# A sparse graph-attention layer: a fifth gather buffer and longer lags between the stages

## The reference

```python
h = jnp.maximum(_layernorm(x), 0.0)                 # x: 8192 x 128 f32
h = h @ W                                           # W: 128 x 128
s_src, s_dst = h @ a[:128, 0], h @ a[128:, 0]
e = leaky_relu(s_src[:, None] + s_dst[None, :], 0.2)
e = jnp.where(adj > 0, e, -9e15)                    # adj: 8192 x 8192 int32, 4 ones a row on average
out = x + softmax(e, axis=1) @ h
```

## Time and profile before

| | us |
|---|---|
| median of 3 timed runs | 804.93 |
| the profiled execution, its span | 858.3 |
| DVE busy | 592.4 (69%) |
| ACT busy | 525.0 (61%) |
| POOL busy | 512.0 (60%) |
| PE busy | 445.4 (52%) |
| adj loads (queue q1), share of the 16 DMA engines | 79.3% |

### The profile page before, as it was taken

The page is one execution under the profiler, slowest core; times in us unless marked ns, Lnnn a source line. Parts: engine busy times, 40 slices in busy tenths (PEclk is TensorE's granted clock), DMA queues, the critical chain, the costliest instruction groups (busy, mean ns, idle before and its releaser), DMA issues.

```text
span 858.3 us, 8941 instructions
## 1 busy us (share of the span) xinstructions
PE 445.4 (52%) x1823; PEld 213.9 (25%) x1855; DVE 592.4 (69%) x3125; ACT 525.0 (61%) x371; POOL 512.0 (60%) x522
## 2 busy tenths in 40 slices
PE   4787555555555546545554545475055567533421
PEld 3652222222222222212122222132022222211221
DVE  7956577777777767566678767767177788755784
ACT  3979777666767667766387777666154877732000
POOL 3745666666656665765655666667636665665571
PEclk9888678677676777766677777777578767765555
DMA  8999999999999999989599999999659799992110
GB/s 339 424 370 419 404 408 408 408 411 407 410 409 409 408 409 405 399 315 393 217 415 411 408 409 408 408 401 409 233 210 394 277 408 409 411 402 92 25 38 11
DMA packets 40903, 299.31 MB, mean 349 GB/s; under 512 B 11052, under 2 KB 14034, under 8 KB 24464
## 3 DMA queue, kind: packets, MB, share of 16 engines
q1 hardware_dynamic: 22976, 276.83, 79.3%
q0 software_dynamic: 15328, 17.58, 6.6%
q10 hardware_dynamic: 2544, 4.33, 1.5%
HBM read 304.31 MB, written 8.65 MB: 365 GB/s over the span
## 4 chain that ended last, share of the span: by engine, by line
DVE 72%; another core or an unknown queue 11%; issue 8%; PE 5%; ACT 2%; DMA 0%; POOLq 0%; DVEq 0%; ACTq 0%
DVE x_all L821 18%; DVE rest L638 5%; DVE words L636 5%; DVE words L640 4%; PE banks L1049 3%; DVE wf L666 2%; DVE top L680 2%; DVE top_bit L662 2%; DVE cand L676 2%; DVE cand L723 1%; DVE one_hot L768 1%; DVE e L785 1%; DVE top_bit L672 1%; DVE top L727 1%
## 5 line engine op out<-in xcount | busy, mean ns | idle before, releaser
L361 POOL DMA_INDIRECT gathered<-table,index x448 | 448.7, 1002 | 295.1 <-DVE index L714 151.4
L467 ACT ACTIVATE mask_buf<-adj_buf,minus_half 128x2048 bf16<-128x2048 int32 x252 | 489.5, 1992 | 141.3 <-issue 56.5
L1049 PE MATMUL banks<-mask_buf,bit_ident 128*128 128x512 bf16 x992 | 316.6, 472 | 37.6 <-issue 24.7
L821 DVE SCALAR_TENSOR_TENSOR x_all<-gathered,weight,x_all 128x128 f32<-128x128 f32 x512 | 157.5, 348 | 16.1 <-DVE x_all L821 7.6
L1049 PEld LDWEIGHTS banks<-mask_buf,bit_ident 128*128 128x128 bf16 x1024 | 113.2, 121 | 203.4 <-issue 137.6
L1061 PE MATMUL banks<-is_wide,before 128*128 128x1 bf16 x64 | 6.9, 176 | 207.9 <-DVE is_wide L751 155.9
L1090 PE MATMUL banks<-x_all,one_hot 128*128 128x128 f32 x128 | 35.4, 368 | 74.1 <-DVE x_all L821 39.0
L481 ACT ACTIVATE prob<-e 128x16 f32<-128x16 f32 x31 | 6.5, 208 | 103.6 <-issue 72.7
L636 DVE MAX8 words<-banks 128x8 f32<-128x512 f32 x64 | 44.3, 693 | 25.4 <-PE banks L1049 18.7
L1061 PEld LDWEIGHTS banks<-is_wide,before 128*128 128x128 bf16 x64 | 4.5, 112 | 227.8 <-DVE is_wide L751 170.8
L640 DVE MAX8 words<-rest 128x8 f32<-128x512 f32 x64 | 44.5, 695 | 2.4 <-DVE rest L638 0.2
(11 more groups left out here) (162 smaller groups left out, 589.4 us busy)
## 6 DMA issues: line engine op xcount, KB each, us to landing
adj_buf<-in_adj SPq DMA_DIRECT2D x128, 2048.0 KB
gathered<-table,index POOLq DMA_INDIRECT x448
table<-gathered ACTq DMA_DIRECT2D x4, 1040.0 KB, 14.0
x_all<-in_x SPq DMA_DIRECT2D x3, 1024.0 KB, 10.8
out<-x_all SPq DMA_DIRECT2D x2, 1280.0 KB
x_all<-in_x SPq DMA_DIRECT2D x2, 512.0 KB, 5.1
out<-x_all SPq DMA_DIRECT2D x1, 1024.0 KB
w_gathered<-table,w_index POOLq DMA_INDIRECT x24
```

The source lines that it names most:

```text
L361: nc.gpsimd.indirect_dma_start(g_cols[buf][:, k, :], None, table, bass.IndirectOffsetOnAxis(index[:, buf, k:k + 1], 0), bounds_check=N, oo ...
L467: nc.scalar.activation(mask_buf[:, u], adj_buf[:, u], ACT.Sign, bias=minus_half[:]).then_inc(mask_ready, 1)
L821: ins = v.scalar_tensor_tensor(at[b], g_view[par][b][:, k, 0:F], weight[:, b, k:k + 1], at[b], ALU.mult, ALU.add)
L1049: ins = mm(bank, bit_ident[:, h * PART_BITS + c], mask_buf[:, u, c * BIT_COLS:(c + 1) * BIT_COLS], start=False, stop=(h == PARTS - 1 and c ...
```

## The change

`BUFS` becomes 5, and a buffer of `gathered` shrinks from 16 to the 14 columns that are used (9100 instead of 8320 floats a partition in all; a memset on POOL clears the 6 columns that the prologue doesn't write). The lags change: counting from i-1 to i-2 (with it `place_wide`), records from i-2 to i-4, the weighted sum from i-3 to i-4, `add_sums` from i-4 to i-5 and from behind unit 0 to behind unit 5. The exponential stays at i-3 and goes from behind unit 2 to behind unit 5. `logits` stay at i-2, with a new wait for the sums that used the buffer of batch i-5 before. The wide gathers go two a batch over five batches, from `GROUP_ENDS[g] + 4` on, and the other wide steps move later. After the loop one more weighted sum and one more `place_wide` are left.

```diff
-BUFS = 4
+BUFS = 5
 LOGITS_LAG = 2
-SUM_LAG = 3
-COUNT_LAG = 1
-RECORD_LAG = 2
-SUMS_LAG = 4
+SOFTMAX_LAG = 3
+SUM_LAG = 4
+COUNT_LAG = 2
+RECORD_LAG = 4
+SUMS_LAG = 5
+WIDE_INDEX_LAG = 4
+WIDE_LOGITS_LAG = 9
+WIDE_SUM_LAG = 11
+WIDE_RUN = 2
...
-        gathered = sb("gathered", [P, BUFS, BATCH * SLOTS * ROW], f32)
+        gathered = sb("gathered", [P, BUFS, COLUMNS * ROW], f32)
...
-            def wide_gather(g):
+            def wide_gather(g, lo=0, hi=MORE + 1):
                 pool.wait_ge(w_index_ready, g + 1)
-                for k in range(MORE):
+                for k in range(lo, min(hi, MORE)):
...
             for i in range(BATCHES):
                 gather_batch(i)
                 for g in range(GROUPS - 1):
-                    if i == GROUP_ENDS[g] + 3:
-                        wide_gather(g)
+                    lo = (i - GROUP_ENDS[g] - WIDE_INDEX_LAG) * WIDE_RUN
+                    if 0 <= lo <= MORE:
+                        wide_gather(g, lo, lo + WIDE_RUN)
             wide_gather(GROUPS - 1)
...
             for i in range(BATCHES):
+                for g in range(GROUPS - 1):
+                    if i == GROUP_ENDS[g] + WIDE_SUM_LAG:
+                        wide_softmax(g)
                 for u in range(FIRST_DONE if i == 0 else 0, UNITS):
                     mask(i, u)
-                    if u == 2 and i >= SUM_LAG:
-                        softmax(i - SUM_LAG)
-                    for g in range(GROUPS - 1):
-                        if u == 5 and i == GROUP_ENDS[g] + 7:
-                            wide_softmax(g)
-                    if u == 6 and i == LAST:
-                        softmax(LAST - 2)
+                    if u == 5 and i >= SOFTMAX_LAG:
+                        softmax(i - SOFTMAX_LAG)
+            softmax(LAST - 2)
             softmax(LAST - 1)
...
                     dve.wait_ge(gathers_done[par], 16 * COLUMNS * (i // BUFS + 1))
+                if i >= BUFS:
+                    dve.wait_ge(sums_added, i - BUFS + 1)
...
-                    if i == GROUP_ENDS[g] + 2:
+                    if i == GROUP_ENDS[g] + WIDE_INDEX_LAG:
                         wide_index(g)
-                    if i == GROUP_ENDS[g] + 6:
+                    if i == GROUP_ENDS[g] + WIDE_LOGITS_LAG:
                         wide_logits(g)
-                    if i == GROUP_ENDS[g] + 7:
+                    if i == GROUP_ENDS[g] + WIDE_SUM_LAG:
                         wide_sum(g)
...
-            weighted_sum(LAST - 3, beside=logits(LAST - 2))
+            weighted_sum(LAST - 4, beside=logits(LAST - 2))
             find_words(LAST, 1)
-            decode(LAST, 1, BATCH, beside=place_wide(LAST - 1))
+            decode(LAST, 1, BATCH, beside=place_wide(LAST - 2))
             make_records(LAST)
-            alone(logits(LAST - 1))
+            alone(place_wide(LAST - 1))
+            weighted_sum(LAST - 3, beside=logits(LAST - 1))
             alone(place_wide(LAST))
...
             for i in range(BATCHES):
-                pack(i, 0)
-                if i >= SUMS_LAG:
-                    add_sums(i - SUMS_LAG)
-                for u in (1, 2):
+                for u in (0, 1, 2):
                     pack(i, u)
                 if i >= RECORD_LAG:
                     add_records(i - RECORD_LAG)
                 pack(i, 3)
                 if i >= COUNT_LAG:
                     count_wide(i - COUNT_LAG)
-                for u in range(4, UNITS):
+                for u in (4, 5):
+                    pack(i, u)
+                if i >= SUMS_LAG:
+                    add_sums(i - SUMS_LAG)
+                for u in (6, 7):
                     pack(i, u)
```

More of the change, by code:

```diff
@@ L101, in gat_kernel @@
         mask_buf = sb("mask_buf", [P, UNITS, PART], bf16)
-        gathered = sb("gathered", [P, BUFS, BATCH * SLOTS * ROW], f32)
+        gathered = sb("gathered", [P, BUFS, COLUMNS * ROW], f32)
         g_cols = [gathered[:, buf, :].rearrange("p (k n) -> p k n", n=ROW) for buf in range(BUFS)]
         g_view = [[g_cols[buf][:, b * OWN:b * OWN + SLOTS, :] for b in range(BATCH)] for buf in range(BUFS)]
-        rows_all = gathered[:, :, :].rearrange("p a (t n) -> p (a t) n", n=ROW)
+        rows_all = gathered[:, :, :].rearrange("p a (t n) -> p (a t) n", n=ROW)[:, 0:TILES, :]
+        spare_cols = gathered[:, :, :].rearrange("p a n -> p (a n)")[:, TILES * ROW:]
         x_all = sb("x_all", [P, TILES, F], f32)
@@ L331, in _ @@
             nc.gpsimd.memset(w_x[:], 0.0).then_inc(iotas, 1)
+            nc.gpsimd.memset(spare_cols, 0.0).then_inc(iotas, 1)
             def normalize(g, par):
@@ L389, in wide_gather @@
                         bounds_check=N, oob_is_err=False).then_inc(w_gathers, 16)
-                nc.gpsimd.indirect_dma_start(
-                    w_x[:, g, :], None, x, bass.IndirectOffsetOnAxis(w_index[:, g, MORE:MORE + 1], 0),
-                    bounds_check=N - 1, oob_is_err=False).then_inc(w_gathers, 16)
+                if hi > MORE:
+                    nc.gpsimd.indirect_dma_start(
+                        w_x[:, g, :], None, x, bass.IndirectOffsetOnAxis(w_index[:, g, MORE:MORE + 1], 0),
+                        bounds_check=N - 1, oob_is_err=False).then_inc(w_gathers, 16)
             def wide_store(g):
@@ L546, in _ @@
             done.add(v.memset(minus_half[:], -0.5))
-            dve.wait_ge(iotas, 6)
+            dve.wait_ge(iotas, 7)
             v.tensor_scalar(ident[:], diff, 0.0, None, ALU.is_equal)
@@ L1112, in _ @@
                     count_wide(i - COUNT_LAG)
-                for u in range(4, UNITS):
+                for u in (4, 5):
                     pack(i, u)
-            add_sums(LAST - 3)
+                if i >= SUMS_LAG:
+                    add_sums(i - SUMS_LAG)
+                for u in (6, 7):
+                    pack(i, u)
+            add_sums(LAST - 4)
+            count_wide(LAST - 1)
+            add_records(LAST - 3)
+            add_records(LAST - 2)
             add_records(LAST - 1)
@@ L1120, in _ @@
             mm(banks[:, 2, 8:9], ones[:], unfit_top[:], start=True, stop=True).then_inc(unfit_summed, 1)
-            for i in range(LAST - 2, BATCHES):
+            for i in range(LAST - 3, BATCHES):
                 add_sums(i)
```

## The result

| kernel | median, us | ratio to before (95%) |
|---|---|---|
| before, timed beside it | 805.05 | |
| after | 817.02 (816.62 to 818.35) | 1.0144 (1.0122 to 1.0166) |

The change costs 12.0 us. The forecast was 792.5 us in a range of 774 to 815, so sign and range were both missed.

What follows compares the result with a forecast made beforehand. Both the loads and DVE's list of work were taken to be near their limit. Wide gathers -13.5 us plus start and tail +1.1 gave -12.4, so 804.9 would become 792.5 us, range 774 to 815.

Steps and rivals of the forecast that it cites:

- The base: Whole kernel: the gain worked out on the 858.3 us profiled execution was taken unchanged off the timed median of 804.9 us.
- (1): Wide gathers on POOL beside DVE: spreading them two a batch removes 29.5 us and adds 16.0, net -13.5 us.
- Removed stalls: Batches around the nine-gather rows: first-gather distances of 34.1, 32.3 and 30.3 us against 22.4, together 29.5 us to win.
- Late gathers: Gathers eleven and up in a row slow DVE's decode; two more per 16-gather batch lose 2.0 us, 16.0 in all.
- The signs that I named for (1): First-gather distances never above 28 us, near 24.4 in batches 14 to 18; decode waits still beginning with the eleventh gather.
- (2): Counting at i-2, records at i-4: PE no longer waits for DVE's is_wide; nothing gained or lost in the sum.
- (3): Exponential behind unit 5, sums at i-4, new wait in logits: ACT gets three units more room, at most 1 us cost.
- (4): Start and tail: batch 3 loses a weighted sum, -5.0 us; tail gains it and a place_wide, +6.1; net +1.1 us.
- E: Timed runs have no such stalls: loads set the loop, only the tail grows by 6.1, 811.0 us; chance 0.17.
- B: Loads are the only limit: all 36.2 us of idle DMA time come back, tail takes 6.1, 774.8 us; chance 0.14.
- D: Pauses between gathers fall under 2.5 us, hitting two batches in four of a group: 824.1 us; chance 0.15.
- C: A gather costs DVE the same at any place, so spreading gains nothing; start and tail stay, 806.0 us; chance 0.10.

Runs made afterwards that it cites:

- second trace: The kernel before, unchanged, profiled a second time: span 803.4 us, timed ratio 1.0005.
- delay_before: The kernel before with 60 extra MAX8 on DVE at the end of batch 15: 826.44 us.
- spread_only: The kernel before with only the wide gathers two a batch, wide scores and sums two batches later: 808.68 us.
- row_of_nine: The kernel after with all nine wide gathers of a group in a row again, lags as changed: 814.51 us.
- sums_back: The kernel after with weighted sums back at i-3, add_sums at i-4, exponential behind unit 2: 811.85 us.
- sums_late: The kernel before with only the fifth buffer, weighted sums at i-4 and add_sums at i-5: 812.52 us.
- counts_late: The kernel before with only counts at i-2, records at i-4, wide steps two batches later, one more place_wide in the tail: 809.64 us.
- wide_sum_30: The kernel before with only the wide exponential and wide sum four batches later, the second group's at batch 30: 806.99 us.
- row_sum_28: row_of_nine with wide scores at +8, wide exponential and sum at +9 (batch 28), exponential behind unit 5: 814.29 us.
- nine_later: The kernel before with the nine wide gathers still in a row but two batches later, wide scores at +8, sum at +9: 808.93 us.
- five_buffers: The kernel before with only the fifth buffer of 14 columns, its memset and the new wait, no lag changed: 806.20 us.

## Why the prediction was wrong, point by point

**The base.** This is the step that failed. The prediction saw that the profiled execution was 53.4 us above the median, said that the timed runs "probably have shorter stalls", and took the whole gain off the median "all the same". All 36.2 us of idle DMA time lay inside that surplus. The second trace has no such stalls (share 1.00), so there was nothing to win back. What made the first execution longer is not shown by anything here.

**(1) Wide gathers, -13.5.** Measured: no gain, and 2.5 to 3.2 us lost, 1.6 to 2.5 of it in POOL's DRAIN, which the sum didn't contain. Removed stalls of 11.7, 9.9 and 7.9 us: in the second trace batch 12 takes 29.9 us by the gathers and batch 13 then 18.3, and 29.9 us is just POOL's own row of 23. The distance between first gathers was no measure of DVE's stall. Late gathers at 2.0 us a batch: nothing (decode 6.6 us beside them). The signs that I named for (1) misled as well: no distance between first gathers is above 24 us in after (I had asked for 28), but those of the ten batches with 16 gathers are 21.0 to 23.5 and not 24.4: the period of the loads.

**(2) Counts and records, 0.** Right for the loop and for the wrong reason: PE's 155.9 us behind `is_wide` were 7.8 us. Not in the sum was the wait of `find_words(31, 0)` behind the moved wide sum, 2.0 us in the trace of after. I had given the wide steps no place of their own in the working; that they end one batch before the tail was to be read from the lags.

**(3) Exponential, sums, new wait, 0.** Right. The room is real (9.9 us of ACT's wait), and worth nothing while DVE waits for PE 56 times. The buffer costs 0.7 us, and its DRAIN is 1.14 us longer.

**(4) Start -5.0, tail +6.1.** The tail was right, 6.0 measured (5.1 and 0.9). The start gave nothing: the first gathers of batch 12 stand at 331.0 in after and 331.4 in before's second trace, and the DMA share is 1.01 from 100 to 300 us in both, so the loads set the early batches too.

**The rivals.** E was the mechanism: loads set the loop, nothing to be had, the tail grows by 6.1. It gave 811.0 and had 0.17. It is 6.0 short: 2.7 for the DRAIN, 2.0 for the wide sum by the trace, and 1.3 that I can't place; the masks ended 2.3 us later in this execution, which is within what executions of one kernel differ by. B and D assumed stalls that don't occur. C (806.0) kept today's price of the wide gathers, but a gather costs DVE nothing in these traces, so there was no price to keep. B also priced a dip at the whole of its idle DMA time, which delay_before shows to be too much. My test for a wrong forecast, that DVE begins to wait for words in most batches, came true (57 times), and was useless: it does so in before as well (56 times).

| term | predicted | measured | by |
|---|---|---|---|
| loop | -13.5 | 0 | spread_only, row_of_nine |
| start | -5.0 | 0 | first gathers |
| one more sum in the tail | +5.0 | +5.1 | sums_back, sums_late |
| one more `place_wide` | +1.1 | +0.9 to 1.0 | after, counts_late |
| wide sum at the end of batch 30 | not in it | +2.0 (1.4 to 3.0), in time 1.4 or nothing | traces, wide_sum_30, row_sum_28 |
| POOL's DRAIN | not in it | +2.7 | trace, nine_later |

## What to carry to other kernels

Before any stall in a trace is priced, its span has to stand where the timed runs stand: here 858.3 against 805, and with a fitting trace (span plus 1.8 us is the time) the same page names the loads as the limit. In a kernel with a software pipeline whose loop runs at the rate of its loads, each stage that is put one step further behind adds its whole work to the end, and slack in the loop pays nothing back as long as nothing disturbs the loop; ask first which stage could move nearer. Look behind the last useful instruction too, since the end of a queue's program can be worth as much as a step of the kernel.

## What the runs showed of the hardware

POOL's DRAIN at the end of the program took 6.84 us in both traces of before and in three variants, 7.98 or 7.99 with a fifth buffer, 9.37 to 9.54 with the wide gathers spread, and 10.27 with four buffers and nine in a row two batches later. It is no sum of these: row_of_nine has the buffer and a later row, and 7.98 us. The timed median moved the same way: by 3.4 us for 3.43 (nine_later), 3.2 for 2.53 (spread_only), 2.5 for 1.56 (row_of_nine against after), 0.7 for 1.14 (five_buffers). What sets the DRAIN is open. An indirect DMA of 128 rows kept POOL 1.00 us with 0.30 us between two in a row, in both traces of before and in after. Beside it DVE's chain of short steps took 6.6 us from MAX8 to L714 in the second trace of before and 11.7 us in the first; why is open.

A busy DMA share did not fix the rate of the loads. At a share of 1.00 to 1.01 the engines moved 396 GB/s from 500 to 700 us in the second trace of before and 405 in delay_before, after its stall. So "the loads set the loop" is a limit that itself moves by 2 to 3%, and no run here shows what moves it.
